# Gathered rows turned five slots apart, and a softmax in parts of 8 and 6 groups, in a two-layer relational graph kernel

## What is computed

```python
def _rgat_layer(h, src, dst, edge_type, W, q, k, b):
    xw = jnp.einsum('nf,rfg->rng', h, W)          # 8 relation matrices
    out_j = xw[edge_type, src]
    out_i = xw[edge_type, dst]
    logits = jax.nn.leaky_relu((out_i @ q + out_j @ k)[:, 0], 0.2)
    alpha = _segment_softmax(logits, dst, n)
    agg = jax.ops.segment_sum(alpha[:, None] * out_j, dst, num_segments=n)
    return agg + b

for l in range(2):
    h = jax.nn.relu(_rgat_layer(h, src, dst, edge_type, W[l], q[l], k[l], b[l]))
x = _layernorm(x + h)
```

## Time and profile before

| | us |
|---|---|
| median of 3 runs | 981.58 |
| lowest, highest | 974.68, 982.33 |
| the profiled execution | 986.6 |
| its span in the trace | 984.5 |

### The profile page before, as it was taken

One profiled execution on the slowest core, in us unless ns is written; L12 is line 12 of the kernel. 1 busy time (PEld: TensorE's weight loads), 2 busy tenths in 40 slices (PEclk: granted clock), 3 DMA queues, 4 the chain that ended last, 5 costly groups with the idle time before them and its releaser, 6 DMA issues.

```text
span 984.5 us, 11352 instructions
## 1 busy us (share of the span) xinstructions
PE 692.9 (70%) x3092; PEld 444.9 (45%) x3092; DVE 808.0 (82%) x2191; ACT 613.8 (62%) x1396; POOL 588.7 (60%) x506
## 2 busy tenths in 40 slices
PE   3546657655664598898888889658899797678830
PEld 2425545444443365564554456434555453334410
DVE  4589997988889787889799999686878879999960
ACT  1569988997798755565557587554556463434440
POOL 4767777777770688888400000088887834876674
PEclk9657876787685599999999999769999897989975
DMA  8266666656554323225344554432222420143210
GB/s 222 83 207 192 200 194 203 200 171 198 174 158 133 99 79 99 84 69 183 114 133 125 162 163 135 140 103 87 68 67 96 157 69 28 48 136 90 64 39 28
DMA packets 87742, 123.00 MB, mean 125 GB/s; under 512 B 14174, under 2 KB 66826, under 8 KB 87679
## 3 DMA queue, kind: packets, MB, share of 16 engines
q1 hardware_dynamic: 69455, 99.35, 32.3%
q0 software_dynamic: 15680, 21.55, 7.8%
q10 hardware_dynamic: 2544, 1.38, 0.6%
HBM read 87.79 MB, written 45.04 MB: 135 GB/s over the span
## 4 chain that ended last, share of the span: by engine, by line
DVE 29%; POOL 23%; issue 18%; PE 10%; ACT 9%; DMA 8%; SPq 1%; POOLq 0%; DVEq 0%; ACTq 0%
POOL xs L461 19%; DVE ys L1121 5%; DVE work L1295 5%; POOL xd L461 4%; PE ps_y L714 4%; ACT stage L795 4%; DMA xs<-h_table,posI 3%; DVE st L1102 3%; DVE ys L1268 2%; DVE opT L1295 2%; DVE st L1071 2%; DMA xs<-x_table,posI 2%; ACT xd L811 2%; DVE st L1061 2%; DVE stage L1065 1%
## 5 line engine op out<-in xcount | busy, mean ns | idle before, releaser
L795 ACT ACTIVATE stage<-stage,nm,rs 128x128 f32<-128x128 f32 x800 | 320.8, 486 | 21.8 <-DVE nm L1056 21.8
L714 PE MATMUL ps_y<-work,wr 128*128 128x512 f32 (+1 forms) x528 | 232.7, 573 | 31.2 <-DVE work L1295 31.1
L461 POOL DMA_INDIRECT xs<-h_table,posI x98 | 132.7, 1354 | 183.9 <-DMA h_table<-ys 154.4
L461 POOL DMA_INDIRECT xs<-x_table,posI x98 | 127.6, 1302 | 62.2 <-DMA x_table<-xd 32.6
L1295 DVE SCALAR_TENSOR_TENSOR work<-typB,xs 128x896 f32<-128x896 uint8 x132 | 142.9, 1087 | 26.3 <-PE ps_y L714 18.9
L714 PEld LDWEIGHTS ps_y<-work,wr 128*128 128x128 f32 x528 | 100.7, 202 | 131.4 <-issue 73.5
L530 POOL DMA_INDIRECT out<-xd,outI x98 | 113.7, 1160 | 61.5 <-issue 28.7
L714 PE MATMUL ps_y<-opT,wr 128*128 128x512 f32 (+1 forms) x256 | 118.4, 588 | 23.7 <-DVE opT L1295 23.7
L461 POOL DMA_INDIRECT xs<-in_x,srcI x98 | 105.6, 1077 | 47.4 <-issue 28.4
L461 POOL DMA_INDIRECT xd<-in_x,dstG x98 | 107.3, 1095 | 29.9 <-issue 29.0
L1061 DVE BATCH_NORM_STATS2 st<-stage 128x6 f32<-128x128 f32 x400 | 82.9, 278 | 19.5 <-DMA stage<-in_x 19.1
(11 more groups left out here) (206 smaller groups left out, 1132.7 us busy)
## 6 DMA issues: line engine op xcount, KB each, us to landing
stage<-in_x SPq DMA_DIRECT2D x39, 640.0 KB, 4.1
out<-stage SPq DMA_DIRECT2D x39, 640.0 KB, 3.0
xs<-alpha_rows SPq DMA_DIRECT2D x28, 448.0 KB, 4.9
x_table<-xd SPq DMA_DIRECT2D x14, 448.0 KB, 3.0
h_table<-ys SPq DMA_DIRECT2D x14, 448.0 KB, 3.7
work<-in_src SPq DMA_DIRECT2D x13, 448.0 KB
ys<-in_edge_attr SPq DMA_DIRECT2D x6, 896.0 KB, 9.0
sameB<-same_rows SPq DMA_DIRECT2D x42, 112.0 KB
```

The lines of the kernel that those rows point to most:

```text
L461: nc.gpsimd.indirect_dma_start(out=buf[:, t, :], out_offset=None, in_=table, in_offset=bass.IndirectOffsetOnAxis(ap=idx[:, t:t + 1], axis= ...
L714: mm = pe.matmul(ps_y[:, u, lo:hi], wr[:, r, :], rows, start=(r == 0), stop=(r == R - 1))
L795: ins = a.activation(slot(c)[:, r, :], slot(c)[:, r, :], ACT.Identity, bias=nm[:, h, n:n + 1], scale=rs[:, h, n:n + 1])
```

## The change

Two numbers of the slot tables. Groups are turned five slots apart instead of four (the last two drawn in by one and two slots), and the first softmax part takes eight groups and not seven. Everything that is worked out from these follows:

```diff
     END = NG * (R - 1)
-    TURN = [0] + [4 * g - 1 for g in range(1, NG)]
-    HA = 7
+    TURN = [0] + [5 * g - 1 - max(0, g - NG + 3) for g in range(1, NG)]
+    HA = 8
     N0 = (TURN[HA - 1] + 4, TURN[NG - 1] + 4)
```

## The result

The changed kernel takes 972.1 us (median of 20 runs), the kernel before 980.35 (20 runs beside them); the ratio of the times is 0.9941, with a 95% interval of 0.9917 to 0.9964. So it is faster, by 0.4 to 0.8%, where 960 and some 2% were forecast: the right way, at a little over a quarter of the size by the ratio. One of the 20 runs of the changed kernel took 1063.3 us and is left out of the ratio.

The account below looks back on a forecast made before the run. Gathers were taken to bound each layer up to the last turn, VectorE from there to the last mask. Layer 0's -14.5 and layer 1's -7.7 us gave -22.2, from 981.6 to 959.4, rounded 960; range for 8 in 10: 944 to 986.

Parts of the forecast that it names:

- B: Each layer's stretch from last turned group to last mask, bound by VectorE: -34.2 us in layer 0, -38.9 in layer 1.
- layer 1: Second layer, to its last scatter: +5.5 us in A, -38.9 in B, +25.7 behind the last mask, together -7.7.
- A: Each layer's stretch from first mask to last turned group: +5.7 us in layer 0, +5.5 in layer 1.
- Its tail: Layer 1 behind its last mask: six groups of scatters follow, 59.2 us and not 33.5, +25.7.
- A of layer 0: First mask to last turn: gathers end it, eleven more slots fit, 152 + 5.7 = 158 us, VectorE at 95%.
- The price of the lock: In A, added masks and shifts on VectorE delay GpSimd's gathers, 0.45 us per wide instruction: 5.7 us.
- The rival of its full price: Each added wide instruction in A delays a gather for its whole length, 14.3 us: 977 us in all, chance 0.12.
- The tail of layer 0: Last mask to last store: four sums in one chain of ScalarE and TensorE, 29 us against 15.2, +14.
- B of layer 0: Last turn to last mask: VectorE's work falls from 119.4 to 87.0 us; at density 0.948, 91.8 us, 34.2 less.
- the slow one: Slots of A take 2.85 us, not 2.55: A is 177 us in each layer, 997 us in all, chance 0.11.
- its ring: Three mask buffers between VectorE and TensorE in A: bursts leave TensorE without a mask, turns leave VectorE without a buffer.
- The 0.18 for "within 1%": Chance of a whole-kernel time within 1% of before: 0.06 from the forecast, 0.12 from the lock's full price.

Follow-up runs that it names:

- the second: The kernel before, profiled once more with no edit: 978.9 us (span 976.9).
- The late copies: Changed kernel with layer 0's copy out and store two slots later for the four groups summed from slot 97 on: 966.2 us, ratio 0.9883.
- both tail edits: Turns five apart, parts of 7 and 7, late copies for the last four groups, idle matmuls in layer 0's tail: 1002.5 us (0.9396), again 990.7 (0.967).

## Why the prediction was right or wrong

- **The mechanism held.** B shrank by nearly what was reckoned (-31.6 of -34.2, -36.0 of -38.9), TensorE's gather waits fell to 1.4 us ("under 5"), and layer 1 came out at -6.7 us against a forecast of -7.7, partly by luck: A was 3.0 us better than forecast and B 2.9 worse. Its tail was right in kind: six groups of scatters, from 3.7 us behind the last mask, and the last one began 59.3 us behind it, in the range of 57 to 62 that I gave. But GpSimd was not "busy throughout" in B: it waited 28.2 us for normalised rows, at the first scatters of most groups down to the ninth, where it had waited 8.9 plus the bulk store.
- **The step that failed is A of layer 0.** I wrote that "the gathers end the stretch in either case", took VectorE's density of B (0.95) for A, and brushed TensorE's 155 us aside, "but those records contain waits". TensorE's own need is about 153, by the run without statistics, and VectorE, at 0.92, adds 8, which TensorE spends waiting for masks (8.8 us): 161.3 us in the profile (161 to 166 in the runs that kept the spacing and both engines' work), against 158. And before, A was 151.7 in my profile and 149.1 in the next one. Together this term is +10 to +12 and not +5.7, the largest single part of the miss: 3.9 of 10.4 us against the first profile, 6.5 of 13.3 against the second. The last gather was issued 16 us ahead of the last turn, so gathers no longer set it at all in layer 0. In layer 1, with less bulk, A was 155.4, better than my 158 (in the other runs 154 to 163).
- **The price of the lock was overstated.** Gathers went from 1338 to 1372 ns on the mean in layer 0, 3.0 us in all against the 5.7 taken. The rival of its full price, 14.3 us, is out. As the gathers weren't the bound, nothing hung on it in layer 0. Nor do the wide instructions carry all the excess, as I had spread it. In the run without the bulk's statistics and shifts, with every mask in place, the 87 gathers took 100.27 and not 119.03 us, 19 less, where nine or ten shifts at 0.45 would be worth 4.
- **The tail of layer 0 was right in kind and short in size:** 32.3 us against 29, inside the 25 to 34 and at the cold end, with links of 7.4 us; of the 32 us that B lost, 17 come back there. The late copies took 6.1 us off it in the trace and 5.9 off the median, which is the best evidence for the chain.
- **B of layer 0** kept 1.6 us more work than reckoned (88.6 and not 87.0), at a density of 0.942 and not 0.948: 94.2 us and not 91.8.
- **The base.** The first profile was some 5 us longer than the second in the phase ahead of the layers. I subtracted from the median and not from it, so this didn't move the forecast, but the profile's A was long too, by 2.6.
- Together: -22.2 + 3.9 (A) + 2.6 (B) + 2.9 (tail) in layer 0, + 1.0 in layer 1, gives the table's -11.8 against the first profile; against the second it is -8.9. Of the rivals, the slow one (2.85 us a slot) was wrong in size: it was 2.60. One half of its ring shows: TensorE waited more for masks (8.8 us and not 2.3). The other doesn't: VectorE waited less for a buffer (2.4 and not 9.8). The 0.18 for "within 1%" was too little for a forecast that is a difference of six large terms, each good to 3 us.

## What to carry to other kernels

When a waited-for engine is relieved, add up what each of the others *needs* in that stretch, one by one; the next bound is at least the largest of these (here 153 us, and 161 measured) and not the old one's share scaled. A busy share of 95% measured where one engine rules doesn't carry over to a stretch where two are full and wait for each other. And work moved from a full loop to behind it is cheap for the engine that did it and dear for the chain that it hangs in: look at the links (here bias, turn, copy, refill, at half the clock), and reorder or keep the clock up there; this gave more than the change did.

## What was not expected

- Seven idle 128-column matmuls between two links kept TensorE's granted clock at 1.00, where it had been 0.50, and cut a link from 5.7 to 3.9 us although they stand in it. The other way round, with 1.5 us a group left out of TensorE's work the clock was 0.92 and not 0.98, and the stretch 9 us longer.
- The kernel before took 978 to 980 us beside most runs, and 1069 and 1034 beside two sets of them, with single slots of other kernels standing for up to 30 us. It isn't a property of one chip: the 1034 were measured on the same chip as medians of 978.5 and 980.3, and one run of the changed kernel took 1063 among 19 of 968 to 979. With turns five apart and both tail edits a kernel took 991 and 1002 there, 30 to 40 more than its like elsewhere and not 55 to 90; why is open.
- Two profiles of the same kernel differ by 7.6 us in span, and nearly all of it lies in two stretches with gathers (first phase 5.0, A of layer 0 2.6). A of layer 1, which gathers too, repeats within 0.3, as do B and the tails.
